# Cross-attention and FFN on one core: three quarters of the output projection moved from the tail into the attention loop

## The reference, cut to what is computed

```python
def xattn(x, cond, Wq, bq, Wkv, bkv, Wp, bp):          # x: 1600 tokens x 512, cond: 5776 keys x 512
    q = (x @ Wq + bq) / sqrt(32)                        # 16 heads of 32
    k, v = split(cond @ Wkv + bkv)
    q, k, v = quantised to 8 bits (v per channel over all keys)
    attn = quantised(softmax(q @ k.T))                  # 16 heads x 1600 x 5776
    return (attn @ v) @ Wp + bp
x = x + xattn(layernorm(x), ctx, Wq, bq, Wkv, bkv, Wp, bp)
x = x + ffn(layernorm(x), w13, w2, norm_w)
# ffn: quantise the row; x1, x3 = split(xq @ w13.T) (2 x 1408); g = relu(x1)^2 * x3;
#      rmsnorm(g) * norm_w; quantise the row; @ w2.T
```

## Time and profile before

| | us |
|---|---|
| median of 3 runs | 1984.74 |
| lowest, highest | 1984.19, 1985.01 |
| the profiled execution | 1991.13 |
| its span | 1989.3 |
| attention loop: first to last exponential begins | 187.7 to 1674.9 |
| tail: last exponential begins to the end | 1674.9 to 1989.3 |

### The profile page before, as it was taken

The page is one execution under the profiler, slowest core; times in us unless marked ns, Lnnn a source line. Parts: engine busy times, 40 slices in busy tenths (PEclk is TensorE's granted clock), DMA queues, the critical chain, the costliest instruction groups (busy, mean ns, idle before and its releaser), DMA issues.

```text
span 1989.3 us, 40167 instructions
## 1 busy us (share of the span) xinstructions
PE 1716.5 (86%) x16046; PEld 1138.5 (57%) x16046; DVE 1670.1 (84%) x2651; ACT 1367.6 (69%) x1299; POOL 1493.8 (75%) x1182
## 2 busy tenths in 40 slices
PE   7997888888788888887888889798988997689996
PEld 6875666665566566555665654344444444467774
DVE  6766999999789999997999999899999996454552
ACT  2445888898678888877888888677777776332221
POOL 1441888898898888888988989888988977255553
PEclk9997999998889999898999995555556555899998
DMA  5575899899989999999899999979777866422311
GB/s 179 204 216 152 183 204 205 188 181 210 208 176 180 199 191 176 194 209 200 175 184 209 180 166 188 189 123 172 154 131 147 148 107 142 142 56 63 78 44 44
DMA packets 862041, 323.09 MB, mean 162 GB/s; under 512 B 789088, under 2 KB 817184, under 8 KB 861856
## 3 DMA queue, kind: packets, MB, share of 16 engines
q1 hardware_dynamic: 861856, 320.53, 77.0%
HBM read 80.87 MB, written 46.20 MB: 64 GB/s over the span
## 4 chain that ended last, share of the span: by engine, by line
DVE 37%; PE 28%; issue 12%; POOL 11%; DMA 5%; ACT 5%; SPq 1%; POOLq 0%; DVEq 0%; ACTq 0%
DVE S L1029 33%; POOL PT L1221 7%; PE PS L626 7%; PE PS L687 6%; DMA PP<-Pr 4%; PE PK L721 3%; PE PK L566 3%; PE PS L593 2%; PE PK L704 2%; ACT Pr L847 2%; PE PK L568 1%; PE PO L645 1%; POOL VQ L1190 1%; PE PO L568 1%; PE PO L566 1%
## 5 line engine op out<-in xcount | busy, mean ns | idle before, releaser
L1029 DVE TENSOR_SCALAR_CACHE_REDUCE S<-PS,SQN 128x1536 f32<-128x1536 f32 (+1 forms) x768 | 1285.6, 1714 | 82.0 <-PE PS L626 66.8
L847 ACT ACTIVATE Pr<-S,MS 128x5888 uint8<-128x5888 f32 x200 | 1041.4, 5207 | 250.3 <-DVE MJ L1048 170.8
L1221 POOL CAST PT<-PP 128x1536 uint16<-128x1536 uint8 (+1 forms) x800 | 1094.4, 1413 | 91.7 <-DMA PP<-Pr 90.2
L626 PE MATMUL PS<-KT,QT 96*128 96x512 bf16 (+1 forms) x2496 | 798.4, 452 | 119.5 <-DVE S L1029 106.4
L645 PEld LDWEIGHTS PO<-VI,PT 128*128 128x128 f16 x9200 | 367.4, 102 | 362.2 <-issue 185.7
L645 PE MATMUL PO<-VI,PT 128*128 128x32 bf16 x9200 | 378.0, 184 | 92.1 <-ACT AO L831 62.8
L626 PEld LDWEIGHTS PS<-KT,QT 96*128 96x128 bf16 (+1 forms) x2496 | 213.3, 108 | 327.5 <-issue 189.8
L566 PE MATMUL PK<-WG,CT 128*128 128x128 f32 (+1 forms) x1272 | 223.8, 307 | 14.4 <-DMA CT<-ctxt 9.7
L568 PE MATMUL PK<-CT,WG 128*128 128x128 f32 (+1 forms) x1272 | 213.1, 296 | 0.0
L566 PEld LDWEIGHTS PK<-WG,CT 128*128 128x128 f32 (+1 forms) x1272 | 175.6, 202 | 17.6 <-issue 13.0
L568 PEld LDWEIGHTS PK<-CT,WG 128*128 128x128 f32 x1272 | 167.5, 195 | 1.8 <-issue 0.6
(11 more groups left out here) (131 smaller groups left out, 1405.0 us busy)
## 6 DMA issues: line engine op xcount, KB each, us to landing
CT<-ctxt SPq DMA_DIRECT2D x180, 256.0 KB, 3.3
k_rows<-KS SPq DMA_DIRECT2D x44, 512.0 KB, 4.1
v_rows<-VS SPq DMA_DIRECT2D x33, 256.0 KB, 3.9
VQ<-v_rows SPq DMA_DIRECT2D x33, 256.0 KB, 3.8
q_rows<-QS SPq DMA_DIRECT2D x13, 512.0 KB, 4.2
W13F<-w13T SPq DMA_DIRECT2D x16, 352.0 KB, 4.2
attn_out<-AO SPq DMA_DIRECT2D x8, 416.0 KB, 4.2
PP<-Pr SPq DMA_TRANSPOSE x200, 5.9
```

Of the source, the lines that this page charges most:

```text
L626: last = pe.matmul(PS[n % 2][p0:p0 + r, f:f + w], QT[h % 3][0:PARTS * HD, q0:q0 + r], KT[h % 3][0:PARTS * HD, c * CHUNK + f:c * CHUNK + f ...
L847: act.activation(Pr[i % 2].rearrange("p t q b -> p t b q"), S[i % 2].rearrange("p (t b q) -> p t b q", b=2, q=P), ACT.Exp, bias=MS[:, i % ...
L1029: v.tensor_scalar(S[i % 2][:, c * CHUNK:c * CHUNK + CW[c]], PS[n % 2][:, 0:CW[c]], neg_step, None, ALU.mult, ALU.min, accum_out=MN[:, i % ...
L1221: gp.tensor_copy(PT[i % 2][:, 2 * t0:2 * t1, :].rearrange("p (t b) q -> p t b q", b=2), PP[i % 2][:, t0:t1, :].bitcast(U8).rearrange("p t ...
```

## The change

Channels 0 to 383 of the attention output (pairs 0 to 5, `DONE_CH`) are complete in DRAM at step 158: `OUT_AT` goes from 11 to 8, so that the sixth pair is stored three steps earlier. In the steps 162, 164, 167, 169, 172, 174, 177, 179, 182, 184, 187, 189 and 192 (`ROWS_AT`, one for each token tile) the loop now takes up a tile:

- SP loads its 384 channels three steps ahead (`load_rows`) and its rows of x one step ahead (`load_x_rows`), and stores the result two steps later (`store_rows`) in a new DRAM tensor `base_rows`.
- PE transposes three 128x128 blocks behind chunk 0 (`rows_turn`). In the next step it makes one f32 product of 128x512 behind chunk 0, two behind chunk 1, and behind chunk 2 a product of the identity with x and a bf16 product of ones with the bias (`rows_product`). For the last tile each of the first three is made twice, with 64 columns each.
- ACT copies the transposed rows out (`rows_turned`) and the sum out of `PK` (`rows_out`), each behind an exponential.
- POOL makes three bf16 parts of the bias (`bias_parts`, three and six instructions), and scales `WP` at closer due times.

Pairs 6 and 7 are no longer stored: `AO` is now one tensor that holds both, 128 channels for each token tile. In the tail PE transposes one block straight from it, makes one product with the last quarter of `WP`, and DVE adds `base_rows` in place of x. The store and the reload of the attention rows, the POOL addition of the bias, and an addition on DVE for the last tile are gone from the tail. `XB` has two buffers there.

```diff
-OUT_AT = 11
+OUT_AT = 8
+DONE_CH = (NG - 1) * GC
+ROWS_AT = [WP_AT + 8 + 5 * t // 2 for t in range(NT)]
...
+            def load_rows(t):
+                if t == 0:
+                    sp.wait_ge(M["s_ao0"], 16 * (H // 4 - 1))
+                    sp.wait_ge(M["s_ao1"], 16 * (H // 4 - 1))
+                if t >= 2:
+                    sp.wait_ge(M["r_tp"], t - 1)
+                sp.dma_start(OL[t % 2], Od[t * P:(t + 1) * P, 0:DONE_CH]).then_inc(M[f"r_ol{t % 2}"], 16)
+            def load_x_rows(t):
+                if t >= 2:
+                    sp.wait_ge(M["r_pr"], t - 1)
+                sp.dma_start(XR[t % 2][0:rows(t), :], x_v[t * P:t * P + rows(t), :]).then_inc(M[f"r_x{t % 2}"], 16)
+            def store_rows(t):
+                sp.wait_ge(M["r_xo"], t + 1)
+                sp.dma_start(Rd[t * P:t * P + rows(t), :], XO[t % 2][0:rows(t), :]).then_inc(M[f"r_st{t % 2}"], 16)
...
-            store_out(H // 2 - 1)
-            sp.wait_ge(M["s_ao0"], 16 * (H // 4))
-            sp.wait_ge(M["s_ao1"], 16 * (H // 4))
...
+            def rows_turn(t):
+                pe.wait_ge(M[f"r_ol{t % 2}"], 16 * (t // 2 + 1))
+                pe.wait_ge(*((M["r_xo"], t) if t else (M["s_kve"], NG * NU)))
+                for k in range(NK - 1):
+                    last = pe.transpose(PK[:, k * P:(k + 1) * P], OL[t % 2][:, k * P:(k + 1) * P], ident[:, :])
+                last.then_inc(M["r_tp"], 1)
+            def rows_product(t, c):
+                n = rows(t)
+                if c == 0:
+                    pe.wait_ge(M["s_wp"], NK)
+                    pe.wait_ge(M["r_ot"], t + 1)
+                if c < 2:
+                    for k in range(c, 2 * c + 1):
+                        for half in range(0, P, n):
+                            pe.matmul(PK[0:n, :], OT[:, k, half:half + n], WP[:, k, :], start=(k == 0 and half == 0), stop=False)
+                    return
...
+                pe.wait_ge(M[f"r_x{t % 2}"], 16 * (t // 2 + 1))
+                pe.matmul(PK[0:n, :], ident[0:n, 0:n], XR[t % 2][0:n, :], start=False, stop=False)
+                pe.matmul(PK[0:n, :], ones[:, 0:n], BP3, start=False, stop=True).then_inc(M["r_pr"], 1)
...
             for i in range(NA + LAG):
...
+                    if c == 0 and i in ROWS_AT:
+                        rows_turn(ROWS_AT.index(i))
+                    if c < 3 and i - 1 in ROWS_AT:
+                        rows_product(ROWS_AT.index(i - 1), c)
...
-                for c in range(NK):
-                    last = pe.transpose(PO[:, c * P:c * P + n], OL[t % 2][0:n, c * P:(c + 1) * P], ident[0:n, 0:n])
-                last.then_inc(M["f_tp"], 1)
+                pe.transpose(PO[:, 0:P], AO[:, t].rearrange("p a c -> p (a c)"), ident[:, :]).then_inc(M["f_tp"], 1)
...
-                    for c in range(NK):
-                        last = pe.matmul(PK[0:n, :], OT[:, c, 0:n], WP[:, c, :], start=(c == 0), stop=(c == NK - 1))
+                    for half in range(0, P, n):
+                        last = pe.matmul(PK[0:n, :], OT3[:, half:half + n], WP[:, NK - 1, :], start=(half == 0),
+                                         stop=(half + n == P))
...
+                if i in ROWS_AT:
+                    rows_out(ROWS_AT.index(i))
+                if i + 1 in ROWS_AT:
+                    rows_turned(ROWS_AT.index(i + 1))
                 if i >= LAG - 1:
                     values_out(i - LAG + 1)
...
-            todo += [(WP_AT + 6 + k, scale_wp, (k,)) for k in range(NK)]
+            todo += [(WP_AT + 6 + k / 2, scale_wp, (k,)) for k in range(NK)]
+            todo += [(WP_AT + 8.15 + part, bias_parts, (part,)) for part in range(2)]
```

More of the change, by code:

```diff
@@ L134, in link, with build @@
         self.sync()
-def build(nc, x, ctxt, ctxl, Wq, bq, Wkv, bkv, Wp, bp, w13T, w2T, norm_w, eye, Qd, Kd, Vd, Od, out):
+def build(nc, x, ctxt, ctxl, Wq, bq, Wkv, bkv, Wp, bp, w13T, w2T, norm_w, eye, Qd, Kd, Vd, Od, Rd, out):
     ctx = ExitStack()
@@ L213, in build @@
         QT.append(tmp("QT2", [NT * P], BF16))
-        AO.append(tmp("AO1", [NT, 2 * HD], F32))
+        AO = tmp("AO", [NT, 2, 2 * HD], F32)
+        OL = ring("OL", 2, [DONE_CH], F32)
+        XR = ring("XR", 2, [C], F32)
+        XO = ring("XO", 2, [C], F32)
+        OT = tmp("OT", [NK - 1, P], F32)
         stage.close()
@@ L470, in _ @@
                     load_v(g, b)
-                if j == OUT_AT and p:
+                if j == OUT_AT and 0 < p < H // 2 - 1:
                     store_out(p - 1)
+                if i + 3 in ROWS_AT:
+                    load_rows(ROWS_AT.index(i + 3))
+                if i + 1 in ROWS_AT:
+                    load_x_rows(ROWS_AT.index(i + 1))
+                if i - 2 in ROWS_AT:
+                    store_rows(ROWS_AT.index(i - 2))
                 if 0 <= i - WP_AT < NK:
@@ L825, in values_out @@
                 act.wait_ge(M["s_pv"], i + 1)
-                if j == 0 and p < 2:
-                    act.wait_ge(M["s_ao"], p + 1)
+                if p == 0 and j == 2 * FULL:
+                    act.wait_ge(M["s_ao"], 1)
                 if j == 0 and p >= 2:
@@ L830, in values_out, with rows_turned, rows_out @@
                 if len(segs) == 1:
-                    act.activation(AO[p % 2][:, j % FULL, (j // FULL) * HD:(j // FULL + 1) * HD], PO[:, 0:HD],
+                    act.activation(AO[:, j % FULL, p % 2, (j // FULL) * HD:(j // FULL + 1) * HD], PO[:, 0:HD],
                                    ACT.Copy).then_inc(M["s_pve"], 1)
                 else:
-                    act.activation(AO[p % 2][0:LAST, FULL, 0:HD], PO[0:LAST, 0:HD], ACT.Copy)
-                    act.activation(AO[p % 2][LAST:P, FULL, HD:2 * HD], PO[LAST:P, HD:2 * HD],
+                    act.activation(AO[0:LAST, FULL, p % 2, 0:HD], PO[0:LAST, 0:HD], ACT.Copy)
+                    act.activation(AO[LAST:P, FULL, p % 2, HD:2 * HD], PO[LAST:P, HD:2 * HD],
                                    ACT.Copy).then_inc(M["s_pve"], 1)
+            def rows_turned(t):
+                act.wait_ge(M["r_tp"], t + 1)
+                if t:
+                    act.wait_ge(M["r_pr"], t)
+                act.activation(OT, PK[:, 0:DONE_CH].rearrange("p (a b) -> p a b", b=P), ACT.Copy).then_inc(M["r_ot"], 1)
+            def rows_out(t):
+                n = rows(t)
+                act.wait_ge(M["r_pr"], t + 1)
+                if t >= 2:
+                    act.wait_ge(M[f"r_st{t % 2}"], 16 * (t // 2))
+                act.activation(XO[t % 2][0:n, :], PK[0:n, :], ACT.Copy).then_inc(M["r_xo"], 1)
             for u in UNITS[-1] + UNITS[0]:
@@ L872, in transposed @@
             def transposed(t):
-                n = rows(t)
                 act.wait_ge(M["f_tp"], t + 1)
```

91 lines of the change are left out of this document (41 added, 50 removed).

## The result

| | before | after |
|---|---|---|
| median, us | 1984.74 | 2004.68 |
| lowest, highest | 1984.19, 1987.62 (5 runs) | 1997.74, 2006.89 (5 runs) |
| ratio | | 1.0089, interval 1.0065 to 1.0113 |
| the profiled execution, its span | 1991.13, 1989.3 | 2006.89, 2005.1 |

A forecast was written before the change was run, and what follows sets the result against it. The prediction took DVE to bound the loop and PE the tail. Tail -26, row work +40 and POOL +3 sum to +17 us on 1984.7, giving 2001.7, range 1973 to 2024.

The forecast's parts named there:

- row work: Loop: transposes and products of 13 tiles on PE make DVE late, 2.9 us a tile, +40 us in all.
- POOL: Loop, around the split of W13: nine bias instructions take 8.6 us, lengthened steps give back 5.8, leaving +3 us.
- steps R + 1: Loop steps with a tile's products, one after its transposes: about 9.5 to 10 us expected; under 8.5 would refute.
- (a): Tail start: the first sum is formed at 1702.95 instead of 1709.46, -6.5 us.
- (b): Tail, second to third turn: only POOL's bias addition leaves the way, -1.2 us.
- (c): Tail, eight full turns: the chain over XI's transpose limits a turn to 16.9 us instead of 19.06, -17 us.
- (d): Tail, last turns: XIF of the last tile is no longer behind PE, -1.5 us.
- E: Tail: end of the up product's second half, where DVE's G starts; XI's transpose is issued 15.3 us later.
- Rival 1: Loop: earlier transposes raise PE's clock before about half the bursts; row work +17, time 1978.7 us; chance 0.16.
- At nothing: Loop: ACT's copies, SP's 39 extra transfers and the earlier store cost 0, bound +5 us.
- rival 2: Loop: PE's clock stays high through all steps, row work costs 0, time 1963 us; chance 0.10.
- rival 3: Loop: PE's clock never rises, row work costs +96, time 2055 us; chance 0.06.

The follow-up runs named there:

- bias_early: The changed kernel with both bias_parts calls due two steps sooner, the second now ahead of POOL's split of W13; ratio 1.0028 to the kernel before.
- xit_first: bias_early with SP's load of base rows and store of a finished tile moved behind the transpose of XI in the tail; ratio 0.9973 to the kernel before.
- no_turn2: bias_early with a tile's three PE transposes replaced by one of 32x32, all products kept; ratio 1.0038 to the kernel before.
- dense: bias_early with the tiles' row work two steps apart, at steps 168, 170 to 192; ratio 1.0090 to the kernel before.
- tail_only: no_turn2 with the loop's f32 products left out and a bias product of 32 columns; ratio 0.9928 to the kernel before.
- all_four: dense with POOL's bias instructions single behind the split, one f32 product behind each of chunks 0 to 2, and xit_first's SP order; ratio 0.9885 to the kernel before.

## Why the prediction was right, and for which wrong reasons

The time was forecast at 2001.7 and came at 2004.68, and the sum of +17 at +15.8 by the spans (+20 by the medians). But that it came so near is luck: two pieces were wrong by 21 us (the row work, too high) and by 16 (POOL and a wait that it made, too low). The forecast held in its direction and in the tail; of its own signs of being wrong, steps R + 1 under 8.5 us, four of the nine full tiles from 170 to 190 showed one.

| term | forecast | measured |
|---|---|---|
| tail, (a) first sum | -6.5 | -8.0 |
| (b) second to third turn | -1.2 | -2.5 |
| (c) eight turns | -17 | -11.4 |
| (d) last turns | -1.5 | -1.5 |
| tail in all (with +0.4 outside of these) | -26 | -23.0 |
| loop, row work on PE | +40 | +18.6 (15.7 + 2.9) |
| POOL | +3 | +7.7 |
| PE's wait for the bias | none | +11.1 |
| before step 161 (scatter; -4.1 in bias_early) | 0 | +1.3 |
| sum | +17 | +15.7 |

- **Tail, (a), (b), (d)**: right, the size of (a) and (b) a little low. Of (a), 1.0 was lost again up to the first `G`, and 0.6 came at the very end.
- **Tail, (c)**: the chain was right, and so was its place: SP issued the transpose at E + 15.3 as forecast (1874.78 for E, 1890.09), and `XIF` is released by its DMA. Mis-sized was the term for the landing: I took 2.47 us from one row at the tail's start; in the turns it took 3.31, 3.46, 3.41 and 2.69, and PE's 15.3 behind it was 15.6. The trace of before had the better number: over its 13 transposes of `XI` the median from issue to landing is 3.2 us. In one of the eight turns some products ran at the lower clock (24 of them in 6.92 us, at a granted clock of 0.75). xit_first shows that the chain "doesn't shrink" only as long as nobody looks at what stands in SP's queue ahead of it.
- **Loop, row work**: the failed step is "I take this for every tile: at the start of the burst the clock is 0.50". It was 0.50 for five of the nine full tiles from 170 to 190. The other four cost 0.7 us, the five 2.2, where I had 2.6 for the burst; the last tile's 3.8. Of the sixteen steps without a burst fourteen gave 0.2 back, and the two with transposes at 0.50 cost 0.5, where I had 0.5 less 0.2 for every tile. The reason that I gave, "since the step before it has only scores and values", was against the trace of before, which has the clock at 1.00 over such work from 1522.8 to 1533.0. Rival 1 named the right size (+17), but its mechanism fell with no_turn2.
- **POOL**: I put its nine instructions at 3, because the lengthened steps of the first tiles would "give POOL that time". Alone, without bursts beside them (dense), they cost up to 7.7 of 8.6, near the upper bound; the three bursts of the stretch then add 2.9 instead of three times 2.9. So the overlap was there, and taken together the two come out near the sum (8.7 + 3 = 11.7 forecast, 60.0 - 49.4 = 10.6 in bias_early). The split of these 10.6 us over the two rows of the table is that of dense.
- **The wait that I overlooked**: I wrote "none of it waits for data: loads are issued one and three steps ahead". That covers loads, not `BP3`, which POOL makes; the prediction counted POOL's work and not who waits for its end. The order in the section on the change shows it: the six instructions stand behind the split, and L692 needs the last of them in step 163.
- **At nothing** was nearly right: tail_only puts copies and transfers at about 2 us from 168 to 194, mostly a `PP` that comes late once, by more than the "up to 1 us" of the prediction.
- Rivals 2 and 3 (clock always up, never up) did not come; all_four comes close to rival 2's 1963 and dense goes towards rival 3.

Still open: why a given burst of after finds the clock up. In after, bias_early, no_turn2 and xit_first it was up for 178 and 188 and down for 175, 180, 185 and 190 each time, but 170, 173 and 183 changed, and 183 did so between bias_early and xit_first (9.25 and 7.69 us), whose loops are the same.
